# Windowed attention on Trainium2: scores per 32 queries with their 160 keys, and turned P in a DRAM raster of 512-byte blocks

## What is computed

```
q, k, v = split(shift_token(x) @ wqkv)             # 8 heads of 64
q, k    = rotary_xpos(l2norm(q) * qs, l2norm(k) * ks)
# windows of 128 queries; keys of the own and the previous window
sim     = einsum('bhwid,bhwjd->bhwij', q * 8, [k of window w-1, k of window w])
mask    = (i < j) | (i > j + 128) | (j == -1)      # each query sees the 128 keys before it and itself
attn    = softmax(where(mask, -max, sim))
x       = x + (attn @ [v of w-1, v of w]) @ wo
x       = x + geglu(layernorm(shift_token(x)) @ w1 + b1) @ w2 + b2
```

## Time and profile before

| what | value |
|---|---|
| median of 3 runs | 4972.72 us (4967.94 to 4975.3) |
| the profiled execution | 4966.22 us |
| its span | 4964.4 us |
| PE busy | 4507.8 us (91%) |
| DVE, ACT, POOL busy | 72%, 60%, 49% |
| granted TensorE clock, mean of the span | 0.959 |
| DMA | 775.96 MB, mean 156 GB/s |

### The profile page before, as it was taken

How to read it: one execution, slowest core, us unless ns; L and a number is a source line. 1 busy time by engine, 2 the same in 40 slices (tenths; PEclk the granted TensorE clock), 3 DMA queues, 4 the chain that set the end, 5 groups by cost and what they waited for, 6 DMA issues and landing times. The chain is left out here.

```text
span 4964.4 us, 269505 instructions
## 1 busy us (share of the span) xinstructions
PE 4507.8 (91%) x107928; PEld 3817.4 (77%) x107928; DVE 3564.7 (72%) x10345; ACT 2979.7 (60%) x8486; POOL 2441.6 (49%) x3196
## 2 busy tenths in 40 slices
PE   7898898678888888666999999999999999999998
PEld 6888888678888888654777777777777777777777
DVE  4666666568878887475777777777777777777775
ACT  5777777534444444354666666666666666666665
POOL 1222222267777777203555555555555555555554
PEclk8999999789999999788999999999999999999999
DMA  2343343467777777694555666555565555555554
GB/s 87 87 96 93 93 98 89 114 143 165 165 165 163 167 164 161 175 299 126 170 170 168 173 174 171 172 171 171 180 196 175 173 173 172 171 171 173 173 175 131
DMA packets 1283528, 775.96 MB, mean 156 GB/s; under 512 B 686800, under 2 KB 1179088, under 8 KB 1282256
## 3 DMA queue, kind: packets, MB, share of 16 engines
q1 hardware_dynamic: 1231888, 700.43, 53.1%
q10 hardware_dynamic: 51392, 73.02, 5.0%
HBM read 410.44 MB, written 362.68 MB: 156 GB/s over the span
## 5 line engine op out<-in xcount | busy, mean ns | idle before, releaser
L2367 ACT ACTIVATE l_prob<-l_prob,l_nb,l_rq 128x256 f32<-128x256 f32 x1024 | 601.6, 590 | 20.8 <-DVE l_nb L2193 13.1
L2033 POOL TENSOR_TENSOR l_prob<-l_prob,l_rinv 128x512 f32<-128x512 f32 x512 | 526.8, 1039 | 108.4 <-DVE l_rinv L2173 108.4
L2017 POOL TENSOR_TENSOR l_k<-l_kn,l_tab 128x512 f32<-128x512 f32 x128 | 162.5, 1270 | 614.8 <-DVE l_kn L2165 614.8
L2559 PE MATMUL lD<-l_hid,w 128*128 128x128 f32 x3072 | 364.0, 275 | 0.0
L2559 PEld LDWEIGHTS lD<-l_hid,w 128*128 128x128 f32 x3072 | 353.3, 192 | 0.0
L2551 PEld LDWEIGHTS lA<-l_hn,w 128*128 128x128 f32 x2048 | 242.9, 195 | 110.1 <-POOL l_hn L2051 61.1
L2202 DVE STREAM_TRANSPOSE l_pb<-l_prob 128x512 f32<-128x512 f32 x512 | 326.6, 676 | 0.6 <-POOL l_prob L2033 0.5
L2027 POOL TENSOR_TENSOR l_qr<-l_q 128x512 f32<-128x512 f32 x128 | 162.4, 1269 | 328.1 <-DVE l_q L2131 328.1
L1097 POOL TENSOR_TENSOR sc_aqx<-sc_late,sc_headmask 128x256 f32<-128x256 f32 x256 | 170.8, 667 | 278.9 <-PE sc_Y L1190 277.2
L1173 PE MATMUL sc_AB<-sc_aq,sc_bkx 32*32 32x32 f32 x16384 | 257.3, 198 | 37.4 <-POOL sc_bkx L1097 29.1
L497 POOL TENSOR_TENSOR rk<-rk,bkraw 128x256 f32<-128x256 f32 x64 | 54.6, 871 | 477.9 <-DVE bkraw L383 477.9
(11 more groups left out here) (276 smaller groups left out, 13707.3 us busy)
## 6 DMA issues: line engine op xcount, KB each, us to landing
scratch_pz<-l_pb SPq DMA_DIRECT2D x256, 512.0 KB, 3.0
l_pT<-scratch_pz SPq DMA_DIRECT2D x1024, 128.0 KB, 3.2
scratch_cm<-cm SPq DMA_DIRECT2D x64, 512.0 KB, 4.1
scratch_qz<-l_q SPq DMA_DIRECT2D x128, 256.0 KB, 2.9
l_qT<-scratch_qz SPq DMA_DIRECT2D x512, 64.0 KB, 2.0
scratch_kz<-l_k SPq DMA_DIRECT2D x128, 256.0 KB, 2.8
l_kT<-scratch_kz SPq DMA_DIRECT2D x512, 64.0 KB, 2.9
sc_early<-scratch_cm ACTq DMA_DIRECT2D x59, 512.0 KB, 4.7
```

The costliest lines, as they stand in the source:

```text
L2017: tt(k1[s][:], kn[s][:], wide(2, slice(0, DH)), ALU.mult)
L2033: tt(prob[s][:, pair], prob[s][:, pair], rinv[s][:, pair].unsqueeze(2).broadcast_to([P, 2, 2 * P]), ALU.mult).then_inc(Q["pn"][s].sem, 1)
L2367: last_ = nc.scalar.activation(prob[s][:, h], prob[s][:, h], ACT.Exp, scale=rq8[s][:, h:h + 1], bias=nb[s][:, h:h + 1], accum_out=sums[s][ ...
L2559: last_ = mm(bank[s][3][:, c * P:(c + 1) * P], w2[:, m, c * P:(c + 1) * P], hid[s][:, m], start=(c == 0 and m == 0), stop=(c == CC - 1 and ...
```

## The change

Scores: for each head, four blocks of 32 queries, each against the 160 keys that it can see. A pair of heads is eight matmuls of 64 rows and 32 columns, each into 32 partitions of the same two banks, 160 columns wide. Exp, row maximum, normalising and the turn of P work on 160 columns per head. The mask is a table of two forms [128, 2, 160] (ordinary, and for the first window of a layer); the masks per stream, remask and the semaphore "prep" are gone.

Keys of the previous window must stand ahead of the own ones, so the turned tile qkT has three slots of 128 tokens for q and k together; the window with w = 0 is put in slot 2, and its k in slot 0 too (four more reads of 64 KB, with a semaphore of their own), the one with w = 1 in slot 1. q and k are turned into one tile and go out in one write of 512 KB and back in four reads with runs of 1 KB, where k's were read before. q's own write and reads are gone. The scores of w = 1 also wait for the copy of k.

P: a query block has 5 blocks of 32 keys. Each partition writes 5 blocks of 512 bytes to its place in a DRAM raster; the distance of two partitions' rows is 9 blocks (4608 bytes), and what is not written stays zero. Four reads per group bring 32 partitions with 8 blocks of 512 bytes each, so that the values see 256 keys as before. The raster is cleared once, by four DMAs of 700 KB at the stage's start, from cleared pT tiles; GpSimd clears qkT (3072 columns), V (1024) and pT (2048) per stream. The values take V's slots in the order of time.

Order: on VectorE the turn of k stands behind inverse sum 1, the turn of pair 0 ahead of deviate, that of pair 1 behind it, then inverse sum 3 and the turns of pairs 2 and 3. rotate_q and rotate_k no longer wait for q_out and k_out. TensorE's queue gets a semaphore increment behind each wait of the scores (4 or 5, 2, 1 and 1 for the four pairs).

```diff
-        wm = one("wm", [P, 2 * P])
+        wm = one("wm", [P, 2, SPAN])
...
-        qT, kT = two("qT", [P, P, NHP]), two("kT", [P, 2, BL, NHP, 32])
-        V, prob = two("V", [P, 2, HEADS, DH]), two("prob", [P, HEADS, 2 * P])
-        pb, pT = two("pb", [P, 2, BL, NHP, 2, 32]), two("pT", [P, 2, BL, NHP, 2, 32])
+        qk, qkT = two("qk", [P, BL, 2, NHP, 32]), two("qkT", [P, 3 * BL, 2, NHP, 32])
+        V, prob = two("V", [P, 2, HEADS, DH]), two("prob", [P, HEADS, SPAN])
+        pb, pT = two("pb", [P, 2, NR, NHP, 32]), two("pT", [P, 2, BL, 2, NHP, 32])
...
-                def write_q(s, u):
+                def write_qk(s, u):
 
                     sp.wait_ge(S["q_turned"][s].sem, S["q_turned"][s].after(u))
                     sp.sem_inc(sems["free"], 1)
-                    sp.wait_ge(S["qT"][s].sem, S["qT"][s].after(u, 1))
+                    sp.wait_ge(S["k_turned"][s].sem, S["k_turned"][s].after(u))
                     sp.sem_inc(sems["free"], 1)
-                    sp.dma_start(a["qz"][s], q1[s][:].rearrange("p h d -> p (h d)")).then_inc(S["q_out"][s].sem, 16)
-
-                def read_q(s, u):
-                    sp.wait_ge(S["q_out"][s].sem, S["q_out"][s].after(u))
+                    sp.wait_ge(S["qkT"][s].sem, S["qkT"][s].after(u, 1))
+                    sp.sem_inc(sems["free"], 1)
+                    if not isinstance(u, int) or u > 1:
+                        sp.wait_ge(S["kT"][s].sem, S["kT"][s].after(u - 1))
+                        sp.sem_inc(sems["free"], 1)
+                    sp.dma_start(a["qkz"][s], qk[s][:].rearrange("p j y h t -> p (j y h t)")).then_inc(S["qk_out"][s].sem, 16)
+
+                def read_qk(s, u, w):
+
+                    sp.wait_ge(S["qk_out"][s].sem, S["qk_out"][s].after(u))
                     sp.sem_inc(sems["free"], 1)
                     sp.wait_ge(Q["sc"][s].sem, Q["sc"][s].after(u * NHP - 1))
                     sp.sem_inc(sems["free"], 1)
+                    turned = a["qkz"][s].rearrange("(i c) (j n) -> j c i n", i=BL, j=BL)
+                    cur = (2, 1)[w] * BL
                     for j in range(BL):
-                        sp.dma_start(qT[s][32 * j:32 * j + 32].rearrange("p (i t) h -> p i (t h)", i=BL),
-                                     a["qz"][s].rearrange("(i c) (j n) -> j c i n", i=BL, j=BL)[j]).then_inc(S["qT"][s].sem, 16)
-
-                def write_k(s, u):
-                    sp.wait_ge(S["k_turned"][s].sem, S["k_turned"][s].after(u))
-                    sp.sem_inc(sems["free"], 1)
-                    sp.wait_ge(S["kT"][s].sem, S["kT"][s].after(u, 1))
-                    sp.sem_inc(sems["free"], 1)
-                    sp.dma_start(a["kz"][s], k1[s][:].rearrange("p h d -> p (h d)")).then_inc(S["k_out"][s].sem, 16)
-
-                def read_k(s, u, w):
-                    sp.wait_ge(S["k_out"][s].sem, S["k_out"][s].after(u))
-                    sp.sem_inc(sems["free"], 1)
-                    sp.wait_ge(Q["sc"][s].sem, Q["sc"][s].after(u * NHP - 1))
-                    sp.sem_inc(sems["free"], 1)
-                    for j in range(BL):
-                        sp.dma_start(kT[s][32 * j:32 * j + 32, w].rearrange("p i h t -> p i (h t)"),
-                                     a["kz"][s].rearrange("(i c) (j n) -> j c i n", i=BL, j=BL)[j]).then_inc(S["kT"][s].sem, 16)
+                        sp.dma_start(qkT[s][32 * j:32 * j + 32, cur:cur + BL].rearrange("p i y h t -> p i (y h t)"),
+                                     turned[j]).then_inc(S["qkT"][s].sem, 16)
+                    if w == 0:
+                        for j in range(BL):
+                            sp.dma_start(qkT[s][32 * j:32 * j + 32, 0:BL, 1].rearrange("p i h t -> p i (h t)"),
+                                         turned[j][:, :, 32 * NHP:]).then_inc(S["kT"][s].sem, 16)
...
-                    sp.dma_start(a["pz"][s, g], pb[s][:, g].rearrange("p j h x t -> p (j h x t)")).then_inc(H[g]["p_out"][s].sem, 16)
+                    n = 32 * NHP
+                    sp.dma_start(bass.AP(a["pz"].tensor, (s * 2 + g) * AREA + (BL - 1) * 32 * n,
+                                         [[(2 * BL + 1) * n, P], [32 * n, NR], [1, n]]),
+                                 pb[s][:, g].rearrange("p r h t -> p (r h t)")).then_inc(H[g]["p_out"][s].sem, 16)
...
-                        sp.dma_start(pT[s][32 * j:32 * j + 32, g].rearrange("p i h x t -> p i (h x t)"),
-                                     a["pz"][s, g].rearrange("(i c) (j n) -> j c i n", i=BL, j=BL)[j]).then_inc(H[g]["pT"][s].sem, 16)
+                        start = (s * 2 + g) * AREA + (j + BL - 1) * 32 * n
+                        sp.dma_start(pT[s][32 * j:32 * j + 32, g].rearrange("p i x h t -> p (i x) (h t)"),
+                                     bass.AP(a["pz"].tensor, start, [[(2 * BL + 1) * n, 32], [BL * 32 * n, 2 * BL], [1, n]])
+                                     ).then_inc(H[g]["pT"][s].sem, 16)
...
-                    write_q(0, 0)
-                    read_q(0, 0)
-                    write_k(0, 0)
-                    read_k(0, 0, 0)
-                    write_q(1, 0)
+                    sp.wait_ge(sems["set"], 1)
+                    for s in range(NB):
+                        for g in range(2):
+                            sp.dma_start(a["pz"][s, g], pT[s][:].rearrange("p g i x h t -> p (g i x h t)")[:, 0:AREA // P]
+                                         ).then_inc(sems["blank"], 16)
+                    write_qk(0, 0)
+                    read_qk(0, 0, 0)
+                    sp.wait_ge(sems["blank"], 16 * 2 * NB)
...
-                        write_k(o, un)
+                        write_qk(o, un)
                     write_p(s, u, 1)
                     read_p(s, u, 0)
                     if within(un):
-                        read_k(o, un, wn)
+                        read_qk(o, un, wn)
...
-                        for t in (kT[s], V[s]):
+                        for t in (qkT[s], V[s], pT[s]):
                             nc.gpsimd.memset(t[:], 0.0)
                         nc.gpsimd.memset(hid[s][:, FULL, :], 0.0)
                         nc.gpsimd.memset(x1[s][1][:], 0.0)
-                        nc.gpsimd.memset(mask[s][0][:], MASKED)
...
-                    if hp == 0 and w == 0:
-                        dve.wait_ge(S["mask0"][s].sem, S["mask0"][s].after(u, 1))
                     nc.vector.memset(pause[:, s:s + 1], 0.0)
                     for x in range(2):
                         last_ = nc.vector.tensor_tensor_reduce(out=prob[s][:, 2 * hp + x], in0=scored(s, hp, x),
-                                                               in1=mask[s][w][:].rearrange("p x n -> p (x n)"), scale=1.0, scalar=3 * MASKED,
+                                                               in1=wm[:, int(u in (0, NW))], scale=1.0, scalar=3 * MASKED,
...
-                    nc.vector.transpose(pb[s][:, g, :, at:at + 2].rearrange("p j h x t -> p (h x) j t"),
-                                        prob[s][:, 2 * hp:2 * hp + 2].rearrange("p h (x j k) -> p (h x) j k", x=2, j=BL)
+                    nc.vector.transpose(pb[s][:, g, :, at:at + 2].rearrange("p r h t -> p h r t"),
+                                        prob[s][:, 2 * hp:2 * hp + 2].rearrange("p h (r k) -> p h r k", r=NR)
...
+                    if within(un):
+                        turn_k(o, un)
                     inverse_sums(s, u, 2)
+                    turn_p(s, u, 0)
                     if mlp:
                         deviate(o, um, wm_)
+                    turn_p(s, u, 1)
...
-                        pe.wait_ge(S["qT"][s].sem, S["qT"][s].after(u))
-                        pe.wait_ge(S["kT"][s].sem, S["kT"][s].after(u))
+                        pe.wait_ge(S["qkT"][s].sem, S["qkT"][s].after(u))
+                        pe.sem_inc(sems["free_pe"], 1)
+                        if w == 1:
+                            pe.wait_ge(S["kT"][s].sem, S["kT"][s].after(u))
+                            pe.sem_inc(sems["free_pe"], 1)
...
-                    for x in range(2):
-                        rows_ = slice(x * DH, (x + 1) * DH)
-                        last_ = mm(scored(s, hp, x), qT[s][rows_, :, hp], kT[s][rows_, :, :, hp].rearrange("p x i t -> p (x i) t"),
-                                   start=True, stop=True)
+                        pe.sem_inc(sems["free_pe"], 1)
+                    own, back = (2, 1)[w] * BL, (1, 0)[w] * BL
+                    for i in range(BL):
+                        for x in range(2):
+                            rows_ = slice(x * DH, (x + 1) * DH)
+                            last_ = mm(scored(s, hp, x)[32 * i:32 * i + 32], qkT[s][rows_, own + i, 0, hp],
+                                       qkT[s][rows_, back + i:back + i + NR, 1, hp], start=True, stop=True)
...
-                            last_ = mm(valued(s, hp)[x * DH:(x + 1) * DH], V[s][:, slot, 2 * hp + x], pT[s][:, g, :, at + x, slot],
```

(9 more changed lines are left out.)

66 lines of the change are left out of this document (24 added, 42 removed).

## The result

The changed kernel takes 5027.0 us (median of 4, 5014.4 to 5033.0) beside 4972.4 (4 runs, 4967.9 to 4975.3): ratio 1.0107, 95% interval 1.0085 to 1.0129. It is slower by 1.1%, where 4910 was forecast. The profiled execution took 5014.4, 48 more than the one of before.

What follows compares the result with a forecast made beforehand. TensorE's queue was taken to bound the local stage, with P's loop through DRAM some 0.4 us behind; 4966.2 - 25 (layer 0) - 38 (layer 1) + 5 (start) = 4908, said as 4910, range 4845 to 5012.

Steps and rivals of the forecast that it cites:

- TensorE's part: Scores on TensorE: two pairs 0.78 us for 1.24, 0.92 less per half (one window of one stream).
- C: Score matmuls: only two of four positions work side by side, TensorE's period stays; 4975, chance 0.15.
- E: Score matmuls: the four blocks of a head go one after another; about 5260, chance 0.06.
- The semaphore increments: Eight or nine more per half on TensorE's queue: taken at 0, from above 0.3 us per half.
- The write: Write of P to DRAM: at about V + 7.0 instead of V + 8.64, reads from V + 9.8.
- V: Time at which the values of pairs 2 and 3 start on TensorE; the loop of P is counted from it.
- The issues: SP's read issues: groups of four keep 2.07 us; in odd halves the last is issued by V + 15.7.
- odd half: Half without the extra k reads: P lands at V + 18.4 to 18.8, under 19.5, so no wait.
- The landing: P's last read lands 2.7 us behind its issue; groups keep 2.07, neither bytes nor block size counting.
- even half: Every second half, four extra k reads ahead of P's second group: +2.07, loop 20.6, over 19.5 by 1.1.
- Rival D: P's 256-run reads cost SP and DMA engines 0.15 us more each; 5000, with later landings 5035; chance 0.16.
- The start: Stage start: more clearing by GpSimd and of DRAM, less the masks; +5 us (0 to +12).

Runs made afterwards that it cites:

- e4: The changed kernel with P read in runs of 2 KB and the k copy made on GpSimd instead of by DMA reads: 4839.7 us.
- e3: The changed kernel with another raster of P, read in 64 runs of 2 KB instead of 256 of 512 bytes: 4910.3 us.
- e1: The changed kernel with the four reads of k into slot 0 issued behind P's second group instead of ahead of it: 4927.5 us.
- e6: e4 with the score matmuls of pairs 0 and 1 issued twice: 5067.4 us.
- e9: The changed kernel with the score matmuls of pairs 0 and 1 run over 256 columns instead of 160, no instruction added: 5011.6 us.
- e10: e4 with the score matmuls of pairs 0 and 1 run over 256 columns instead of 160, no instruction added: 4854.9 us.

## Why the prediction was wrong

**TensorE's part: right.** Two pairs of scores were to take 0.78 (0.70 to 0.86) and took 0.71; the positions work side by side, rivals C and E are out. In e4, where TensorE is all but the bound, the period is 19.4 to 19.6 in layer 0 (forecast 19.5) and 19.6 to 19.9 in layer 1 (19.95). The values rows were the right witness against the rule of the Trainium skill ("TensorE: Matmul & The Clock Gate", "The mechanism") in its strict reading, that a weight load overlaps matmuls in flight only where the row group differs: here four matmuls of one row group, in four column blocks, start within 0.05 us.

**The semaphore increments: not quite 0.** The idle time of TensorE's loads ahead of lB's scores with nothing to wait for was 66 us in 228, it was 39.9 in 231 before; some 0.2 us per half, within the 0.3 given from above. Whether the increments or the new shape of the scores make it was not tried apart; e4's periods, at or under the forecast, leave no room for a cost.

**The write: right.** V + 7.0 was forecast, it was V + 6.84 (3010.23 to 3017.07). The reads began at V + 9.63 (3019.86; forecast 9.8). Normalise 0.72, turn 0.50, exp 0.51 (0.70, 0.46, 0.52).

**The issues: right.** The last read was issued by V + 15.9 in the odd half (forecast 15.7) and V + 17.9 in the even one (17.7).

**The landing: here it failed.** The step is "I keep 2.07: the k reads, half the bytes in blocks of 512 bytes, took as long as the P reads, so neither bytes nor block size shows in it", and the landing of 2.7 behind the last issue that was kept with it. (The 2.7 was right for the kernel before, 2.8 in the median of its trace.) 2.07 is the pace at which SP issues. It nearly stayed (2.55 and 1.91 from group to group), and an issue of P's reads is 0.45 us in the median where it was 0.43. But how soon SP can issue does not say how soon the DMA engines serve. They were at 0.98 and then at 1.12 to 1.23, from the first read until 3028.2, where the burst before had room behind its first group (0.97, then 0.86). P landed at V + 20.1, 4.2 after the last issue ended, and not at V + 18.6. In the even half it was V + 21.3, 3.4 after the last issue, and not 20.6. So the odd half, which was to have 0.9 us to spare, had a wait of 0.9, and the even one 2.1.

The row could not carry the conclusion drawn from it. A k read of 64 KB in blocks of 512 bytes and a P read of 128 KB in blocks of 1 KB are 128 packets each: bytes and block size differed, the number of packets was the same. It is that number which the change doubled, to 256 per read of P. Rival D read the same rows the other way.

So it is rival D in place and mechanism, but not in part of its price: the blocks cost at the DMA engines, and next to nothing at SP's issue. D gave 5000 and with landings 0.3 later 5035; measured was 5027. That this is near is partly luck: D had the even loop at 21.8 and the odd one at 19.9, and had no term for the clock. Its chance was set at 0.16 because the issue pace, which the trace showed, was read as the service pace, which it doesn't show. e3 is the test: the same bytes and the same issues in a quarter of the packets give back 117 us, the place of the k copy in the queue gives 100 (e1), and short reads with the copy off the queue 187 (e4).

What was not settled: e3 makes the runs longer and also puts them closer together in DRAM. Which of the two counts was not tried apart. And q's reads, 256 KB, used to run early in a half; they now stand in the burst ahead of P's second group, as one half of each joint read. The forecast gave the doubled bytes no price ("2.07 as before"). No run puts them back, so their share in the late landing is open.

**A term left out: the clock.** A wait of 2 us can cost more than 2 us. Behind the one that ended at 3072.76 the granted clock went from 1.00 to 0.53 and back (windows, PEclk is the third from last):

```profile
3072.00:3074.00 2.00, 1.24 (x32) 1.07 (x40) 0.27 (x3) 0.10 (x1) 1.92 (x3) 1.00 0.34 91
3074.00:3077.00 3.00, 3.00 (x42) 2.52 (x27) 1.68 (x13) 3.00 (x12) 1.02 (x2) 0.53 0.00 0
3077.00:3080.00 3.00, 3.00 (x15) 2.04 (x14) 1.56 (x5) 1.31 (x6) 1.32 (x3) 0.90 0.00 0
```

0.53 is about the lower of the two levels, 1.2 GHz. The output projection took 3.39 us there instead of 2.05, and that period, from first values group to first values group, was 22.57. Periods of the same place in layer 0 at full clock are 21.1 in the median (5 of them), those with the fall 22.65 (10): a fall costs some 1.5 us. The wait of 2.13 that ended at 3051.60 did not do it, so it is not sure each time. Adding up, over the local stage from 2331 us to 80 us before the end, the stretches at the lower level times the share of the clock that was missing gives 34 us in the change, 0 in the kernel before and in e4, 3 to 5 in e1 to e3. So the clock falls where the waits for P are near 2 us, and goes away with them. The Trainium skill ("TensorE: Matmul & The Clock Gate", "HAM oscillation — how this bites in real kernels") describes kernels that lose the clock to gaps in TensorE's work; the trace agrees. The prediction counted waits at their length.

**The start: right.** +5 was forecast; the first values group of the stage stood 3.5 us later. The first period behind it was 25.96 for 21.72, which is counted with the loop below.

**The balance.** Profiled against profiled, +48: 127 periods of 21.07 in the mean for 20.72 are +44.5, the start +3.5. Forecast was -63 and +5. Of the difference of 108 in the loop 34 are the clock. The other 74 are the landing in the main, by an estimate from the rows above: against the forecast the odd half is 0.6 longer in layer 0 (20.1 for 19.5) and 0.15 in layer 1 (20.1 for 19.95), the even one 0.7 in both (21.3 for 20.6), which makes 67 over 127 halves and leaves 7.

## What to carry to other kernels

The pace at which a queue issues DMAs says nothing of how fast they are served: read the engines' share while the burst runs, and where it stands near 1, price an added or split packet at the landing of what is last in the queue. Before concluding from two rows that a size does not matter, ask what else was equal in them; here it was the number of packets. Put first what is needed first, and let scattering and gathering share the small blocks, so that not both the write and the read are made of them. A shorter engine is worth only as much as the loop beside it has slack, and a wait of 2 us on TensorE can bring the slow clock with it: experiments on such a kernel measure the clock too, so compare granted clocks before dividing a difference by the number of halves.

## What was not expected of the hardware

A loop on TensorE seems to outgrow what is kept of its instructions: with 16 more matmuls per half it stopped for 3 to 5 us per turn (24 stops, 96 us in e6; 302 instruction loads for 71). An experiment that doubles work by doubling instructions can measure this instead; making the instructions longer (e9, e10) does not. A DMA share of 1.23 in a window of 2 us stood with 199 GB/s, and one of 0.97 before with 314 GB/s: a high share is not a high rate when the packets are small.
